# A four-stage graph network on one core: the layer norms' inverse root shortened, gain and shift moved to ScalarE, and buffers of their own for the last two blocks of relation products

## The reference

```
deg_isqrt = deg ** (-0.5)
x = ln(x + L0(x))   # ten hops of h = 0.9 * norm * segment_sum((h*norm)[src]) + 0.1 * h0
x = ln(x + L1(x))   # two graph attention layers, 4 heads of 64, each relu(_ln(gat(...), g, be)), then @ Wo + bo
x = ln(x + L2(x))   # h = einsum('nd,rdo->rno', x, W); (x @ W0 + segment_sum(h[type, src] * weight)) / deg
x = ln(x + L3(x))   # attention over edges, Wo, batch norm, feed-forward, batch norm

def _ln(x, g, b):
    m = x.mean(-1, keepdims=True)
    v = x.var(-1, keepdims=True)
    return (x - m) / jnp.sqrt(v + EPS) * g + b
```

## Time and profile before

| | us |
|---|---|
| median of 3 runs (3343.50 to 3345.42) | 3344.31 |
| the profiled execution | 3343.69 |
| its span in the profile | 3342.1 |

### The profile page before, as it was taken

How to read it: one execution, slowest core, us unless ns; L and a number is a source line. 1 busy time by engine, 2 the same in 40 slices (tenths; PEclk the granted TensorE clock), 3 DMA queues, 4 the chain that set the end, 5 groups by cost and what they waited for, 6 DMA issues and landing times.

```text
span 3342.1 us, 42848 instructions
## 1 busy us (share of the span) xinstructions
PE 2121.1 (63%) x14275; PEld 1836.6 (55%) x14276; DVE 2169.4 (65%) x5824; ACT 1245.1 (37%) x1339; POOL 1816.3 (54%) x1791
## 2 busy tenths in 40 slices
PE   2875999999999456666456666643333344554455
PEld 1554999999999344444344444423333333544444
DVE  7997776766768466767567888863433335555555
ACT  1886766676675333333223333310000003222222
POOL 2333222222222577777477777727777767777771
PEclk7987999999999667777677788766666666666667
DMA  2100000000000644444345555422222224444441
GB/s 64 25 1 1 0 0 0 0 0 0 0 0 2 195 131 139 141 139 135 97 136 149 150 153 151 136 66 52 59 59 58 59 57 125 133 132 136 133 121 36
DMA packets 133729, 264.99 MB, mean 79 GB/s; under 512 B 33994, under 2 KB 77622, under 8 KB 133510
## 3 DMA queue, kind: packets, MB, share of 16 engines
q0 software_dynamic: 72208, 188.45, 20.9%
q1 hardware_dynamic: 24678, 50.78, 4.8%
q10 hardware_dynamic: 36692, 23.93, 2.3%
HBM read 235.41 MB, written 27.85 MB: 79 GB/s over the span
## 4 chain that ended last, share of the span: by engine, by line
POOL 33%; DVE 13%; issue 12%; PE 8%; DMA 1%; ACT 1%; ACTq 0%; POOLq 0%; DVEq 0%
POOL t_rows L2200 12%; POOL t_rows L2621 11%; POOL t_rows L2955 10%; DVE t_rows L2400 3%; PE t_sum_ps L2308 2%; DVE t_own L1988 2%; DVE t_onehot L2127 1%; PE t_product_ps L1934 1%; PE t_sum_ps L2642 1%; PE t_sum_ps L3015 1%; DMA t_rows<-rel_table_b,t_rel 0%; DMA t_rows<-kv_table_b,t_src 0%; PE t_small_ps L2994 0%; DVE t_so_far L2371 0%; DVE y_fast L2420 0%
## 5 line engine op out<-in xcount | busy, mean ns | idle before, releaser
L2200 POOL DMA_INDIRECT t_rows<-gat_table,t_src x806 | 770.2, 956 | 327.3 <-issue 242.5
L1238 PE MATMUL hop_ps<-parts,wide 128*128 128x256 f32 x5900 | 713.9, 284 | 4.1 <-DVE parts L1334 2.8
L1238 PEld LDWEIGHTS hop_ps<-parts,wide 128*128 128x128 f32 x5900 | 711.2, 192 | 6.1 <-issue 3.6
L1289 ACT CAST wide<-counts 128x3200 fp32r<-128x3200 fp8e4 x177 | 506.3, 2863 | 230.9 <-PE hop_ps L1238 211.4
L2308 PE MATMUL t_sum_ps<-t_rows,t_onehot 128*128 128x264 f32 x1660 | 466.1, 449 | 101.6 <-DVE t_rows L2400 101.6
L1299 POOL CAST wide<-counts 128x3200 fp32r<-128x3200 fp8e4 x59 | 168.7, 2859 | 580.7 <-PE hop_ps L1238 564.7
L2621 POOL DMA_INDIRECT t_rows<-rel_table_b,t_rel x403 | 385.0, 955 | 181.4 <-issue 179.9
L2308 PEld LDWEIGHTS t_sum_ps<-t_rows,t_onehot 128*128 128x128 f32 x1660 | 370.2, 227 | 181.3 <-issue 104.7
L2955 POOL DMA_INDIRECT t_rows<-kv_table_b,t_src x403 | 384.1, 953 | 137.0 <-issue 121.2
L2642 PE MATMUL t_sum_ps<-t_rows,t_onehot 128*128 128x128 f32 x830 | 151.2, 366 | 291.6 <-DMA t_rows<-rel_table_b,t_rel 291.6
L2642 PEld LDWEIGHTS t_sum_ps<-t_rows,t_onehot 128*128 128x128 f32 x830 | 147.0, 279 | 300.6 <-issue 297.9
(11 more groups left out here) (452 smaller groups left out, 3318.7 us busy)
## 6 DMA issues: line engine op xcount, KB each, us to landing
t_dst_wide<-dst_row SPq DMA_DIRECT2D x72, 544.0 KB, 4.1
t_rows<-gat_table,t_src POOLq DMA_INDIRECT x806
rel_table_b<-t_stage ACTq DMA_DIRECT2D x25, 512.0 KB, 3.4
t_rows<-rel_table_b,t_rel POOLq DMA_INDIRECT x403, 2.5
t_rows<-kv_table_b,t_src POOLq DMA_INDIRECT x403
gat_table<-t_own ACTq DMA_DIRECT2D x10, 520.0 KB, 4.3
kv_table_b<-t_fresh ACTq DMA_DIRECT2D x5, 512.0 KB, 2.9
out<-x SPq DMA_DIRECT2D x6, 256.0 KB
```

Of the source, the lines that this page charges most:

```text
L1238: last = nc.tensor.matmul(ps[bank][0:columns.shape[-1], 0:2 * D], columns[:, k, :], parts[old][:, k, :], start=(k == 0), stop=(k == NB - 1))
L1289: nc.scalar.copy(wide[b % B][:, :, :], column(b)).then_inc(widened, 1)
L2200: c.nc.gpsimd.indirect_dma_start(t.rows[:, slot(k), 0:FW], None, self.table, bass.IndirectOffsetOnAxis(ap=t.src[:, k:k + 1], axis=0)).then ...
```

## The change

Four edits. (1) `inverse_root` forms its first guess in one multiply-add on the bits of the variance (by -0.5) and the scaled variance in one fused instruction on variance and guess: two instructions where there were four, of which one pair was not chained. It is called in every norm: in the hops, in Enter, in both layers, behind layer 2, in the relations, and four times at the finish. (2) Gain and shift leave DVE; they are loaded as two columns for each layer (`t.gains`, one feature per partition) and are the scale and bias operands of ACT's relu on the transposed rows. (3) The relation products of blocks 23 and 24 go into buffers of their own, `self.spare`, in the part of `t.rows` behind the relations' ring; MIXED_EARLY falls from 18 to 16, so that the mix of blocks 16 and 17 moves from block 22 of layer 2 into the relations. (4) To make room, the relations' ring has three blocks in place of four.

```diff
+SPARE_STAGES = 2
...
-    v.tensor_scalar(scaled, var, 0.5, None, ALU.mult)
-    then(v.tensor_scalar(tmp.bitcast(i32), var.bitcast(i32), 1, None, ALU.arith_shift_right))
-    then(v.tensor_scalar(root.bitcast(i32), tmp.bitcast(i32), -1.0, float(0x5F3759DF) - 2.0 ** 31, ALU.mult, ALU.add))
-    then(v.tensor_tensor(scaled, scaled, root, ALU.mult))
+    then(v.tensor_scalar(root.bitcast(i32), var.bitcast(i32), -0.5, float(0x5F3759DF) - 2.0 ** 31, ALU.mult, ALU.add))
+    then(v.scalar_tensor_tensor(scaled, var, 0.5, root, ALU.mult, ALU.mult))
...
-        pairs = [(t.params[:, i, j, :], spread(d[f"L1_gnn_{m}{n}"], HID)) for i, n in enumerate("12") for j, m in enumerate(("b", "g", "be"))]
+        pairs = [(t.params[:, i, :], spread(d[f"L1_gnn_b{n}"], HID)) for i, n in enumerate("12")]
+        pairs += [(t.gains[:, i, j:j + 1], d[f"L1_gnn_{m}{n}"].rearrange("(p o) -> p o", o=1)) for i, n in enumerate("12") for j, m in enumerate(("g", "be"))]
...
-        c.nc.scalar.activation(t.turned_x[:, i % 2, 0:m], t.pt[0:HID, 0:m], ACT.Relu).then_inc(self.copied, 1)
+        c.nc.scalar.activation(t.turned_x[:, i % 2, 0:m], t.pt[0:HID, 0:m], ACT.Relu, bias=t.gains[:, layer.number, 1:2], scale=t.gains[:, layer.number, 0:1]).then_inc(self.copied, 1)
...
+        at = REL_RING * CAP * D
+        self.spare = t.rows[:, :, :].rearrange("p s f -> p (s f)")[:, at:at + SPARE_STAGES * NREL * D].rearrange("p (s f) -> p s f", s=SPARE_STAGES)
+
+    def staged(self, b):
+
+        if b >= NB - SPARE_STAGES:
+            return self.spare[:, b - (NB - SPARE_STAGES), :]
+        return self.t.stage[:, b % STAGES, :]
...
-            act.wait_ge(self.tabled[b % STAGES], 16 * (b // STAGES))
-            act.wait_ge(self.mixed, b - STAGES + 1)
+            if b < NB - SPARE_STAGES:
+                act.wait_ge(self.tabled[b % STAGES], 16 * (b // STAGES))
+                act.wait_ge(self.mixed, b - STAGES + 1)
...
-MIXED_EARLY = NB - STAGES
+MIXED_EARLY = NB - STAGES - SPARE_STAGES
...
-            then(norm_set(c, then, t.norm, blocks, lambda b: t.hidden[:, b, 0:HID]))
-            then(v.tensor_tensor(at, at, gain, ALU.mult))
-            v.tensor_tensor(at, at, shift, ALU.add).then_inc(self.normed, 1)
+            norm_set(c, then, t.norm, blocks, lambda b: t.hidden[:, b, 0:HID]).then_inc(self.normed, 1)
...
-REL_RING = 4
+REL_RING = 3
...
-                if b >= REL_RING and k == (b + 1) * CAP - 1 and shared(b):
+                if b >= REL_RING and k == (b + 1) * CAP - 1 and shared(b - REL_RING):
```

More of the change, by code:

```diff
@@ L1622, in __init__ @@
         self.shared = c.sem("t_shared")
-        self.params = sb("params", [P, 2, 3, HID])
+        self.params, self.gains = sb("params", [P, 2, HID]), sb("gains", [HID, 2, 2])
         self.wo, self.bo = sb("wo", [HID, D]), sb("bo", [P, D])
@@ L1862, in act @@
             act.wait_ge(self.done, SETS[i - 2][-1] + 1)
-        c.nc.scalar.activation(t.turned_x[0:HID, i % 2, 0:m], t.pt[0:HID, 0:m], ACT.Relu).then_inc(self.copied, 1)
+        c.nc.scalar.activation(t.turned_x[0:HID, i % 2, 0:m], t.pt[0:HID, 0:m], ACT.Relu, bias=t.gains[:, layer.number, 1:2], scale=t.gains[:, layer.number, 0:1]).then_inc(self.copied, 1)
         for b in blocks:
@@ L1977, in dve_last @@
         for j, b in enumerate(blocks):
-            dve.wait_ge(self.tabled[b % STAGES], 16 * (b // STAGES))
+            if b < NB - SPARE_STAGES:
+                dve.wait_ge(self.tabled[b % STAGES], 16 * (b // STAGES))
             dve.wait_ge(self.x_done, 3 * blocks[0] + 2 * j + 2)
-            self.c.nc.vector.tensor_copy(t.stage[:, b % STAGES, 4 * D:NREL * D], t.pr[1][:, 0:4 * D]).then_inc(self.x_out_dve, 1)
+            self.c.nc.vector.tensor_copy(self.staged(b)[:, 4 * D:NREL * D], t.pr[1][:, 0:4 * D]).then_inc(self.x_out_dve, 1)
     def mix(self, dve, b):
@@ L1987, in mix @@
         for r in range(NREL):
-            last = v.scalar_tensor_tensor(total, t.stage[:, b % STAGES, r * D:(r + 1) * D], t.own_rel[:, r, b:b + 1], total, ALU.mult, ALU.add)
+            last = v.scalar_tensor_tensor(total, self.staged(b)[:, r * D:(r + 1) * D], t.own_rel[:, r, b:b + 1], total, ALU.mult, ALU.add)
             then(last)
@@ L2035, in act_late @@
                 act.wait_ge(self.x_done, k + 1)
-                to = t.stage[:, b % STAGES, lo * D:hi * D] if n < 2 else t.own[:, b, 0:D]
+                to = self.staged(b)[:, lo * D:hi * D] if n < 2 else t.own[:, b, 0:D]
                 c.nc.scalar.copy(to, t.pr[k % 2][:, 0:(hi - lo) * D]).then_inc(self.x_out, 1)
             act.wait_ge(self.x_out, 3 * b + 3)
-            act.dma_start(rows[b * P:(b + 1) * P, :, :], t.stage[:, b % STAGES, :].rearrange("p (r f) -> p r f", r=NREL)).then_inc(self.tabled[b % STAGES], 16)
+            act.dma_start(rows[b * P:(b + 1) * P, :, :], self.staged(b).rearrange("p (r f) -> p r f", r=NREL)).then_inc(self.tabled[b % STAGES], 16)
     def dve(self, dve, layer, i):
@@ L2420, in close @@
             then(v.tensor_reduce(hid, own.rearrange("p (h f) -> p f h", h=HEADS), AX, ALU.add))
-            then(v.scalar_tensor_tensor(hid, hid, 1.0 / HEADS, t.params[:, self.number, 0, :], ALU.mult, ALU.add))
+            then(v.scalar_tensor_tensor(hid, hid, 1.0 / HEADS, t.params[:, self.number, :], ALU.mult, ALU.add))
         def norm(i):
             blocks = SETS[i]
-            at = t.hidden[:, blocks[0]:blocks[-1] + 1, 0:HID]
-            gain, shift = (t.params[:, self.number, j, :].rearrange("p (o f) -> p o f", o=1).to_broadcast([P, len(blocks), HID]) for j in (1, 2))
-            then(norm_set(c, then, t.norm, blocks, lambda b: t.hidden[:, b, 0:HID]))
-            then(v.tensor_tensor(at, at, gain, ALU.mult))
-            v.tensor_tensor(at, at, shift, ALU.add).then_inc(self.normed, 1)
+            norm_set(c, then, t.norm, blocks, lambda b: t.hidden[:, b, 0:HID]).then_inc(self.normed, 1)
         make_hots(0)
```

6 lines of the change are left out of this document (3 added, 3 removed).

## The result

| | us |
|---|---|
| kernel before, median of 4 runs (3342.74 to 3345.42) | 3343.9 |
| changed kernel, median of 4 runs (3316.71 to 3319.62) | 3317.74 |
| ratio, with its 95% interval | 0.9922 (0.9905 to 0.9939) |
| the changed kernel's profiled execution, its span | 3318.56, 3316.9 |

The forecast was 3323.3, from 3319.5 to 3331.0. The sign held, and most of the mechanisms, but the gain was 26.2 us (25.1 from one profiled execution to the other) where 21.0 were forecast, and the time lies under the range. Timed again later, the changed kernel (e13) stood 28.2 us under the kernel before beside it (3318.56 against 3346.72). The question is where 4 to 5 us more came from.

The account below looks back on a forecast made before the run. POOL's gathers were taken to bound layer 1 and the relations, the DVE, PE and ACT loop layer 2. Terms 1.4 + 1.5 + 6.2 + 2.9 + 1.0 + 6.5 + 0.1 + 0.3 + 1.1 = 21.0 us gave 3323.3, range 3319.5 to 3331.0.

Parts of the forecast that it names:

- The root: Each shorter inverse root on DVE saves 0.28 us: 1.4 in the last hop, 1.1 in the finish, 0.3 in the relations.
- Gain and shift: In the layers' norms, taking the pair off DVE saves 0.88 us for four blocks, about 0.76 for three, 0.62 for two.
- the relu: On ACT between PE's transposes and product, two operands from memory cost between 0 and 0.2 us; 0.2 taken.
- The clock behind it: Layer 2's five full sets: less PE idle time raises its clock, cutting DVE's waits for Wo's product by 2.9 us, bounds 0 and 4.
- Layer 2 up to block 22, the sum: Layer 2's first gather to block 23's lift: loop 6.2, clock 2.9, two-block set 1.0 and mix 6.5, forecast 16.6 us.
- Block 22, the mix: Layer 2, block 22: moving the mix away gains 6.5 us, since block 23's scan and the whole tail wait behind it.
- The last set: Layer 2's last set: gain and shift worth nothing behind PE's late products, relu costs 0.2, root gives 0.28: 0.1 us.
- The buffers: Own buffers for blocks 23 and 24 remove no wait and only permit moving the mix: 0 us.
- Moved mix: About 6.2 us of mix work at two relations blocks hides in DVE's idle time: 0 us.
- ring of three: In the relations, three blocks in place of four do not stall POOL's gathers: margin 30 us, cost 0.
- relations, finish: One root at the end of the relations gives 0.3 us, four in series in the finish give 1.1.
- Rivals B to E: B gathers cancel gain, 3332.4, 0.09; C mix unhidden, 3329.5, 0.08; D new wait, 3329.8, 0.04; E ring stalls, 3348.9, 0.03.

Follow-up runs that it names:

- e13: The changed kernel unchanged, profiled and timed again: 3318.56 us, ratio 0.9918 to the kernel before.
- e15: The kernel before, unchanged, profiled again; the kernel before stood at 3346.72 us in that round.
- e8: Kernel before plus 16 added PE products of 128 columns ahead of each four-block set's transposes: 3341.14 us, ratio 0.9991.
- e1: Changed kernel with the mix of blocks 16 and 17 put back at block 22 of layer 2: 3325.16 us, ratio 0.9940 to the kernel before.
- e16: The changed kernel unchanged, a further profile: its execution took 3322.99 us.
- e6: Kernel before plus 76 added PE products of 68 columns in its idle time ahead of block 23's lift: 3367.27 us, ratio 1.0067.
- e7: Changed kernel plus added PE products at three idle places: four-block sets, block 23's lift, last set's x: 3322.49 us, ratio 0.9939 to the kernel before.
- e11: Changed kernel plus 10 added PE products of 128 columns ahead of the turn of the last set's x: 3315.08 us, ratio 0.9913 to the kernel before.
- e5: Kernel before with only the own buffers and the ring of three, mix still at block 22: 3344.68 us, ratio 1.0002.

## Why the forecast missed, step by step

- **The root, 0.28.** Right. In the hops DVE's last instruction ended 2.58 us after PE's last product before, 2.59 in e15, and 1.21 and 1.20 in the changed kernel and e13: 1.38 for five roots, 0.276 each. The rule that the forecast weighed (the Trainium skill, "VectorE: DVE Perf Modes", section "The DRAIN you can't avoid": a semaphore costs nothing extra) would have given 2.0 and is not borne out here. The rows, before and after:

```profile
1083.21 0.34 DVE L1356 SCALAR_TENSOR_TENSOR x<-cut_first,c_h,x 53x128 f32<-53x128 f32 x1
```

```profile
1082.37 0.34 DVE L1356 SCALAR_TENSOR_TENSOR x<-cut_first,c_h,x 53x128 f32<-53x128 f32 x1
```

- **Gain and shift, 0.88, and the relu, 0.2.** The relu cost 0.185. Layer 1 gave 2.1 over all profiles where 1.5 was forecast; the forecast put the clock at nothing there, and the product of the two-block set, 1.79 to 1.90 us in five of seven profiles before, took 1.15 to 1.47 with the edits.
- **The clock behind it, 2.9.** Right in size in layer 2 and shown as a cause. The five waits were 2.32, 2.60, 2.92, 2.25 and 2.25, together 12.3; 0.93 of them is the slower relu, so 14.4 - 11.4 = 3.0 is the clock. e8 gained 3.9 in the same waits by PE's activity alone. The reason given, "the shorter the idle time was, the higher the clock", holds only roughly: 3.16 us of idle time was followed by 0.81 before, 2.63 by 0.76 after.
- **Layer 2 up to block 22, the sum.** 1.6 to 1.9 short. Alone the mix gave 6.6, the roots 4.8 and gain and shift 5.0, 16.4 in all and close to the 16.6 forecast; together they gave 18.2 to 18.5. About 2 us thus appear only when the edits meet (POOL's wait fell by 11.0 where 9 were forecast). More than half of them appear where the two norm edits meet: e1, with both and with the mix in its old place, gained 11.0 to the lift (537.7 against 526.7), where the two alone make 9.8 and 10.1 were forecast. Why has not been settled.
- **Block 22, the mix, 6.5.** Right, 6.6 and 7.5. The rows and the gathers of block 23 and 24 were there.
- **The last set, 0.1.** This step failed. It took the late products as they stood in the trace and asked only what stands ahead of the transposes; their own length, 3.90 at a clock of 0.57, and that of block 23's sums ahead of them, 6.93 with the first 5.4 us at 0.50, were taken as fixed. They were 2.37 and 5.7 in two of three profiles of the changed kernel. In the third, e16, with the long rows, the stretch from the lift to the turn of the last x took 35.9 us, as in both profiles of the kernel before, in place of 33.4: there the forecast's 0.1 held. The term should have been a chance: 0.1 or about 2.7.
- **The buffers, 0.** 0.1 to 0.7 us between the last product and the first gather, under what the times can tell.
- **Moved mix, ring of three, relations, finish.** Right: 506.1 and 505.8 for the relations, 1.4 for the last stretch. Rivals B to E did not come.
- **The range.** Its low end allowed 3 us for three terms that were sized well and nothing for terms that were taken as zero. With 2.2 for the tail and 1.9 more for the loop the sum would have been 3319.3. Of the last 1.6 us to 3317.74, 0.6 may be layer 1's, and the rest no stretch shows: the mean gain of the profiles is 24.9 us, that of the medians 26.2.

## What to carry to other kernels

A TensorE row read at half clock is not a fixed cost: where the chain passes such a row, list it with its price at either level, and give the change a chance of moving it, in either direction. Between two executions of one program 2.6 us may switch in one place, so take several profiles of an unchanged program before a cause is named for a difference of that size. Where PE idles behind a norm and wide products follow on the path, some filler products that end as the norm does bring those products to full clock (2.5 us here by the profiles; 2.7 and 1.6 by the times), while a few too many cost as much as they bring.

## What the runs showed of the hardware

- A granted clock of 0.50 held through 32 us in which PE was never idle (e6, products of 68 columns), and rose 5 us into the sums of 264 columns behind. In e7 products of the same 68 columns ran for 6.42 us at a clock of 1.00 throughout. What makes the difference is not shown.
- The fillers of e11 (128 columns) began at 1.00, ran on at 0.50 from 0.7 us into them, and the clock rose as they ended: 0.59 over them, 0.99 behind.
- The same program had the clock at 1.00 over 2.95 us of PE's idle time in one execution (the changed kernel's first) and over 2.92 in another (e16). Behind it the clock stayed up in the first and fell to 0.58 over the next 1.9 us in the second, with PE busy.
- Stores of 0.5 MB out of two places in SBUF ran at about 290 and at about 350 GB/s (e5).
- Seven dependent passes of DVE with one tensor of 128x128 as input took 1.80 us, 0.26 each, where those of the mix, with two, took 0.39 each.
